# Value products of two key tiles in a row, with a third slot of probabilities

## The reference

```python
x = L0_attn_encoding                                    # 4 x 1024 x 128
xn = _layernorm(x)
x = x + causal_attention(xn, R) + mixture16(xn)         # one head; 16 experts, 2 per token
xn = _layernorm(x)
x = x + attention16(xn) + block(xn)

def attention16(x):                                     # 16 heads of width 8, no mask
    scores = q @ k.T / sqrt(8)
    attn = softmax(scores)                              # over all 1024 keys
    return (attn @ v) @ w_o
def block(x):                                           # 16 heads of width 4, causal,
    x = x + causal_heads(rmsnorm(x)) @ w_up             # then a mixture of 8 experts
    return x + mixture8(rmsnorm(x))
```

## Time and profile before

| | |
|---|---|
| median of 3 runs | 2106.05 us (2105.44 to 2109.2) |
| profiled execution: its own time on the page (span, first to last instruction) | 2106.5 us |
| PE busy | 2004.6 us, 95% |
| DVE busy | 1449.5 us, 69% |
| ACT busy | 1212.8 us, 58% |
| POOL busy | 248.6 us, 12% |
| mean granted clock of TensorE | 0.970 |

### The profile page before, as it was taken

One profiled execution on the slowest core, in us unless ns is written; L12 is line 12 of the kernel. 1 busy time (PEld: TensorE's weight loads), 2 busy tenths in 40 slices (PEclk: granted clock), 3 DMA queues, 4 the chain that ended last, 5 costly groups with the idle time before them and its releaser, 6 DMA issues.

```text
span 2106.5 us, 37548 instructions
## 1 busy us (share of the span) xinstructions
PE 2004.6 (95%) x14520; PEld 956.8 (45%) x14520; DVE 1449.5 (69%) x2024; ACT 1212.8 (58%) x2207; POOL 248.6 (12%) x376
## 2 busy tenths in 40 slices
PE   6989999999999999999899999999989999999899
PEld 3753233344765523344566542334456633334455
DVE  6758887673777688766577778876357888867232
ACT  2341677777442367788544156778864266777621
POOL 0022000000013300000002310000003300000034
PEclk9987999999999999999999999999999999999989
DMA  5244101000155010010116301001005310000011
GB/s 195 67 129 111 28 7 32 25 18 3 61 152 123 16 31 16 27 31 5 35 49 186 80 7 31 16 18 33 3 26 150 91 26 14 29 19 17 2 51 40
DMA packets 66643, 105.29 MB, mean 50 GB/s; under 512 B 11137, under 2 KB 20417, under 8 KB 66081
## 3 DMA queue, kind: packets, MB, share of 16 engines
q1 hardware_dynamic: 66464, 102.90, 17.7%
HBM read 79.13 MB, written 22.94 MB: 48 GB/s over the span
## 4 chain that ended last, share of the span: by engine, by line
PE 83%; DVE 7%; ACT 3%; issue 2%; DMA 2%; SPq 2%; POOL 1%; POOLq 0%; ACTq 0%; DVEq 0%
PE ps L1835 19%; PE ps L1805 16%; PE ps L1760 10%; PE ps L1669 8%; PE ps L1705 7%; PE ps L1695 7%; PE ps L1764 4%; DVE row_max L1295 2%; PE ps L1846 2%; PE ps L1747 2%; DVE row_max L1299 1%; PE ps L1620 1%; PE ps L1608 1%; ACT prob L1508 1%; PE ps L1584 1%
## 5 line engine op out<-in xcount | busy, mean ns | idle before, releaser
L1508 ACT ACTIVATE prob<-ps 128x512 f32<-128x512 f32 (+1 forms) x1664 | 854.7, 584 | 283.6 <-PE ps L1805 227.1
L1295 DVE TENSOR_REDUCE row_max<-ps 128x1 f32<-128x1024 f32 x512 | 606.6, 1219 | 123.1 <-PE ps L1760 121.5
L1805 PE MATMUL ps<-q_stack,k_stack 96*128 96x512 bf16 (+4 forms) x1792 | 493.5, 366 | 12.2 <-ACT prob L1508 6.9
L1835 PE MATMUL ps<-prob,v_ones 128*32 128x512 f32 (+3 forms) x4608 | 463.1, 477 | 2.6 <-ACT prob L1508 0.8
L1760 PE MATMUL ps<-k_stack,q_stack 96*128 96x512 bf16 x1024 | 320.6, 398 | 11.9 <-DVE row_max L1295 10.4
L1299 DVE TENSOR_REDUCE row_max<-ps 128x2 f32<-128x1024 f32 (+3 forms) x256 | 258.6, 1021 | 83.2 <-PE ps L1764 51.0
L1805 PEld LDWEIGHTS ps<-q_stack,k_stack 96*128 96x128 bf16 (+1 forms) x1792 | 140.7, 96 | 324.8 <-ACT prob L1508 190.7
L1448 ACT ACTIVATE prob<-ps 128x512 f32<-128x512 f32 x146 | 87.0, 597 | 345.3 <-PE ps L1695 341.2
L1008 POOL TENSOR_TENSOR prob<-prob,spread_w 128x512 f32<-128x512 f32 x144 | 187.1, 1300 | 540.8 <-DVE prob L1180 247.1
L1669 PEld LDWEIGHTS ps<-wd,prob 128*128 128x128 f32 (+1 forms) x1600 | 208.1, 193 | 73.7 <-issue 52.4
L1669 PE MATMUL ps<-wd,prob 128*128 128x128 f32 (+1 forms) x1600 | 213.9, 278 | 6.2 <-POOL prob L1008 6.2
(11 more groups left out here) (178 smaller groups left out, 1598.7 us busy)
## 6 DMA issues: line engine op xcount, KB each, us to landing
spread_w<-scratch_r SPq DMA_DIRECT2D x128, 128.0 KB, 2.9
spread_w<-scratch_r SPq DMA_DIRECT2D x64, 256.0 KB, 3.3
k_stack<-scratch_k SPq DMA_DIRECT2D x48, 256.0 KB, 6.4
q_stack<-scratch_q SPq DMA_DIRECT2D x48, 256.0 KB, 7.1
scratch_k<-tmp SPq DMA_DIRECT2D x36, 256.0 KB, 4.2
k_stack<-scratch_k SPq DMA_DIRECT2D x96, 64.0 KB, 2.3
q_stack<-scratch_q SPq DMA_DIRECT2D x96, 64.0 KB, 2.3
scratch_k<-tmp SPq DMA_DIRECT2D x36, 128.0 KB, 2.6
```

Source lines behind the costliest of these rows:

```text
L1295: dve.tensor_reduce(nm[G % 2][:, t, j], ring_pair(r)[:], AX_X, ALU.max).then_inc(s["ring_used"], 1)
L1508: act.activation(to, src, ACT.Exp, scale=SCALES[kind_of(G)]).then_inc(s["p_ready"], 1)
L1805: ins[n] = pe.matmul(dst[n][:, to], keys(G, head)[:, kc * P:(kc + 1) * P], queries(G, head)[:, lo:hi], start=k == 0, stop=True, skip_group ...
L1835: ins = pe.matmul(bank(V_BANK)[CW * j:CW * (j + 1), first - at:end - at], v_st[G % 2][:, kc, j, :], p_slot(v, j)[:, first - at:end - at], ...
```

## The change

1. `SLOTS_P = 3`: `prob` gets a third slot, and quads take the slots 0, 2, 1 in turn, counted from the batch's first quad. Exponentials of quad v wait for the value products of quad v-3 in place of v-2.
2. The four `spread_w` tiles no longer have memory of their own; they lie in the third slot (`SPREAD_SLOT`). The first four loads of a mixture that run behind a batch's heads wait for the last value product that read that slot.
3. Value products of full heads are placed two quads at a time: quad 2n and 2n+1 together, once the exponentials of both are there (`follows`). In the planner the second costs no fixed 0.19.

```diff
+SLOTS_P = 3
+SPREAD_SLOT = 2
 def values_time(kind, q, part):
     lo, hi = values_parts(kind, q)[part]
-    return 0.19 + (hi - lo) * 1.7e-3
+    return (0.0 if follows(kind, q) else 0.19) + (hi - lo) * 1.7e-3
+def follows(kind, q):
+    return kind == 0 and q % 2 == 1
+def slot_of(v):
+    return (0, SPREAD_SLOT, 1)[(v - QUAD0[PER * batch_of(group_of_quad(v))]) % SLOTS_P]
+def slot_free_at(v):
+    return max(v - SLOTS_P + 1, QUAD0[PER * batch_of(group_of_quad(v))])
...
-                if G in ready and quads.index((G, q)) < len(values_end) + 2:
+                if G in ready and quads.index((G, q)) < len(values_end) + SLOTS_P:
...
-                if not (opens and evacuating):
-                    starts["values"] = max(exp_end[G, q], staged[-1] if opens else 0.0) + LAT
+                last_of = q + 1 if (G, q + 1) in quads and follows(kind_of(G), q + 1) else q
+                if not (opens and evacuating) and (G, last_of) in exp_end:
+                    starts["values"] = max(exp_end[G, last_of], staged[-1] if opens else 0.0) + LAT
...
+                more = True
+                while more:
...
+                    more = False
+                    if part == len(values_parts(kind_of(G), q)):
+                        part = 0
+                        values_end.append(pe)
+                        more = (G, q + 1) in quads and follows(kind_of(G), q + 1)
...
-        prob = sb("prob", 2 * GH * HALF)
-        p_slot = lambda v, j: prob[:, (v % 2 * GH + j) * HALF:(v % 2 * GH + j + 1) * HALF]
+        prob = sb("prob", SLOTS_P * GH * HALF)
+        p_slot = lambda v, j: prob[:, (slot_of(v) * GH + j) * HALF:(slot_of(v) * GH + j + 1) * HALF]
-        spread_w = [sb(f"spread_w{n}", HALF) for n in range(SPREADS)]
+        spread_w = [prob[:, (SPREAD_SLOT * GH + n) * HALF:(SPREAD_SLOT * GH + n + 1) * HALF] for n in range(SPREADS)]
...
+                if which == 0 and b >= 2 and i < SPREADS:
+                    sp.wait_ge(s["pv_done"], max(v for v in range(QUAD0[PER * (b - 1)]) if slot_of(v) == SPREAD_SLOT) + 1)
...
-                if v >= 2:
-                    act.wait_ge(s["pv_done"], v - 1)
+                if slot_free_at(v) > 0:
+                    act.wait_ge(s["pv_done"], slot_free_at(v))
```

More of the change, by code:

```diff
@@ L123, in values_time, with group_of_quad @@
     lo, hi = values_parts(kind, q)[part]
-    return 0.19 + (hi - lo) * 1.7e-3
+    return (0.0 if follows(kind, q) else 0.19) + (hi - lo) * 1.7e-3
+def follows(kind, q):
+    return kind == 0 and q % 2 == 1
+def group_of_quad(v):
+    return int(np.searchsorted(QUAD0, v, side="right")) - 1
+def slot_of(v):
+    return (0, SPREAD_SLOT, 1)[(v - QUAD0[PER * batch_of(group_of_quad(v))]) % SLOTS_P]
+def slot_free_at(v):
+    return max(v - SLOTS_P + 1, QUAD0[PER * batch_of(group_of_quad(v))])
 def maximum_time(cols):
@@ L288, in windows @@
             elif what == "values":
[L289 to L298 removed]
+                more = True
+                while more:
+                    G, q = quads[len(values_end)]
+                    half, kc, lo, hi = QUADS[kind_of(G)][q]
+                    self.add("values", G, q, part)
+                    pe += values_time(kind_of(G), q, part)
+                    part += 1
+                    more = False
[3 more added lines that the diff above has]
+                        more = (G, q + 1) in quads and follows(kind_of(G), q + 1)
+                        if (G, q + 1) not in quads or QUADS[kind_of(G)][q + 1][0] > half:
+                            evacuating.append((pe, G, half))
             elif what == "piece":
@@ L1007, in spread @@
                 pool.wait_ge(s["down_done"], k - 1)
-                pool.tensor_tensor(hid[k % 2][:], gu[k % 2][:], spread_w[load % SPREADS][:], ALU.mult).then_inc(s["hid_ready"], 1)
+                pool.tensor_tensor(hid[k % 2][:], gu[k % 2][:], spread_w[load % SPREADS], ALU.mult).then_inc(s["hid_ready"], 1)
             for what, *how in plan.of("POOL"):
@@ L1193, in spread @@
                     dve.wait_ge(s["down_done"], k - 1)
-                dve.tensor_tensor(hid[k % 2][:], gu[k % 2][:], spread_w[load % SPREADS][:], ALU.mult).then_inc(s["hid_ready"], 1)
+                dve.tensor_tensor(hid[k % 2][:], gu[k % 2][:], spread_w[load % SPREADS], ALU.mult).then_inc(s["hid_ready"], 1)
             added, attended = [0] * B, [0] * B
```

18 lines of the change are left out of this document (4 added, 14 removed).

## The result

The changed kernel takes 2141.98 us, median of four runs (2135.15 to 2147.93), against 2107.62 for the kernel before, measured beside it: 1.0158 times as long, 95% interval [1.0141, 1.0175]. It is slower by 34 us where 18 were forecast, and 2 us above the end of the range. The profiled execution is the fastest of the four: 2135.15 us, 26.9 us more span than before. (A run's time is some 1.8 us longer than its span, here 2135.15 against 2133.4; the span of the kernel before, 2106.5, is compared with spans alone.) Its mean granted clock is 0.971; the others, at 0.967, 0.966 and 0.963, took 2140.60, 2143.36 and 2147.93. The 45 runs of the kernel before that stand beside the experiments lie between 2104.6 and 2114.6 at 0.969 to 0.975.

The account below looks back on a forecast made before the run. PE was taken as the bound, with little slack on DVE. Full-head terms 9.9 - 0.5 + 8.6 + 1.7 - 1.9, others 0, gave +17.8 us on a median of 2106.05: 2124 us, range 2100 to 2140.

Parts of the forecast that it names:

- The mechanism and the full heads: Full heads: a joint block of 1.86 us leaves DVE without pieces, and PE then waits for it; +17.8 us.
- the interval: Full heads, commonest stretch from one paired block to the next: 5.87 us against 5.66 before, +0.21 each.
- Outputs: Full heads, eight intervals whose output transposes take ring slots and wait for DVE: 6.74 us, +0.42 each.
- three pieces: Full heads, nine intervals with three pieces and seven units: 4.95 us against 5.01, -0.5 us together.
- The eight other intervals with outputs: Full heads, remaining intervals with output transposes: +0.70 us for four and +0.61 for four.
- The rule on weight loads: Joined blocks: unhidden loads, 108 ns per pass, would take 28 of 30.7 us saved; the prediction found the trace disagreed.
- Rival 1: Whole kernel: PE stays the bound and the ring never makes it wait; 2076 us, chance 0.09.
- Rival 3: Full heads: ACT's exponentials bind in place of DVE, 5.61 us with the piece first; 2100 us, chance 0.07.
- Rival 2: Full heads lose 17.8 us, but the mixed stretch (-9.6) and causal heads (-8) give it back; 2106 us, chance 0.17.
- Rival 4: Holes also open in the mixed stretch (+8.4) and causal heads (+8), beyond full heads; 2140 us, chance 0.12.
- Full units with causal pieces: Group 4 and the end of group 3, 40 pairs: DVE and PE level, 0 taken; ends -9.6 and +8.4 us.
- The third slot and causal heads: Causal heads: exponentials may run a quad further; 0 taken from PE's small gaps, ends -8 and +8 us.

Follow-up runs that it names:

- e3: The changed kernel with causal heads planned with two slots instead of three; 1.0171 times the kernel before.
- e8: The changed kernel with the last piece and last unit before a pair of value blocks swapped, 53 times; 1.0143 times the kernel before.
- e10: The changed kernel without pairs in group 4 of a batch, third slot planned everywhere; 1.0168 times the kernel before.
- e11: The changed kernel with pairs and third slot planned only in groups 1 to 3 of a batch; 1.0106 times the kernel before.
- e9: The changed kernel's memory, planned without pairs, third slot planned only in groups 5 and 6 of a batch; 1.0072 times the kernel before.
- e12: The changed kernel's memory, planned without pairs, third slot planned only in group 5 of a batch; 1.0001 times the kernel before.
- e6: The changed kernel with exponentials of full heads over 256 of 512 columns, maxima whole; 1.0113 times the kernel before.
- e7: The changed kernel with full heads' maxima over 512 of 1024 columns and exponentials over 256 of 512; 0.9864 times the kernel before.
- e4: The changed kernel with maxima of full heads over 512 of 1024 columns; 0.9967 times the kernel before.
- e2: The changed kernel planned without pairs, third slot kept in the plan for all groups; 1.0062 times the kernel before.
- e5: The kernel before with maxima of full heads over 512 of 1024 columns; 0.9953 times the kernel before unedited.

## Why the prediction was right or wrong

**The mechanism and the full heads: right, and shown.** The working gave 5.87 for the interval; the trace has 5.88. Outputs: 6.74 expected, 6.74 measured; three pieces 4.95, and 4.96. The eight other intervals with outputs (+0.70 and +0.61, given without their length) measure 7.80 and 6.79. The timeline of one with outputs:

```profile
292.70 0.59 PE L1834 MATMUL ps<-q_stack,k_stack 96*128 96x512 bf16 x2
293.63 0.63 PE L1875 MATMUL ps<-const_f,tmp 128*128 128x128 f32 x4 [0.33 <-DVE row_max L1324]
...
296.28 1.07 PE L1864 MATMUL ps<-prob,v_ones 128*32 128x512 f32 x8
```

The +17.8 for all of these stands against +18.9 in groups 1 to 3 of this execution, and 19.9 to 21.0 in e3, e8, e10 and e11. That 18.9 comes so near is partly luck: in these groups the changed execution ran 20.4 us at the lower level, the one before 30.6, and at 0.33 us for each, as in e9 and e12 (2.2 for 6.8), 3 us of loss are hidden by it. In the first batch, where e3, e6 and e10 have as much of it as before, the three groups lose 4.5, or 18.1 in four batches; with 0.33 put back for each us that is missing, the changed kernel, e3, e10 and e11 all come to 22, of which the kernels without pairs show up to 1.7 by themselves. The intervals are right, then, and the sum is short by 0 to 4 us that no run places. The block behaved as worked out: PE's next matmul comes 1.86 after its start (283.66 to 285.52), so the entry and the exit of one block were saved. The rule on weight loads in the Trainium skill (TensorE: Matmul & The Clock Gate, What overlaps and what doesn't), that they overlap matmuls in flight only where the row group differs, would make the block some 2.08 (an estimate: 1.86 and two loads of 108 ns); the trace disagrees again, and e7's 5.41 leaves no room for it.

**Rival 1, PE stays the bound: refuted.** e7 shows that its 5.41 is there when maxima and exponentials take less time, e4 that the maxima are what stood in the way. **Rival 3, ACT: refuted as the bound** by e6, but its number was good: it gave 5.61 where ACT alone binds and the piece is first, and e4 shows 5.64. **Rival 2, the hole is given back in the mixed stretch and causal heads: refuted**; these parts added 9.4 us instead of taking 17.6 away. **Rival 4, holes in the mixed stretch and causal heads too:** its 2140 is the number nearest to the result, and that is chance. Group 4 added 2.1 where it has 8.4; the 7.3 behind it are near its 8, but causal heads have no pairs and so no such holes; its sum would be 34 in one execution, and 26.9 were measured.

**Full units with causal pieces: 0 was forecast.** Group 4 adds 2.1, inside the bounds of -9.6 and +8.4. In e10 and e11, without pairs in it, it adds 1.8: the pairs themselves cost 0.3 there, as good as the 0 of the forecast, and the rest is there without them.

**The term that was mis-sized: "The third slot and causal heads", taken as 0.** Alone it measures +9.6 + 4.5 = +14 (e2), beyond the +8 that I gave as its end; in the changed kernel groups 5 to 8 and the mixtures add 7.3. The step that failed was to take the value from PE's small gaps before, "nearest to the small gaps of the first stretch", as though a freer planner could only use gaps up. A third slot changes which work is done first: units before pieces, so that the maxima of the batch's last group end later, and there a chain of 8 us has to be covered by what is left. That chain was in the trace of before, at 478.68 to 486.59, and PE was covered to 0.6 us of it. e2 and e9 show this loss. In the changed kernel it is there too, smaller: the loads of group 8's first unit wait 1.23,

```profile
490.85 0.10 PEld L1834 LDWEIGHTS ps<-q_stack,k_stack 48*128 48x128 bf16 x2 [1.23 <-DMA q_stack<-tmp]
```

and group 7 adds 0.77 per batch. More of the 7.3 lies in group 5, 1.2 per batch, of which e11, with the order of before there, still has 0.45; what makes the rest no run shows.

**The second part of the miss is the clock.** The sum was made against one execution and moved to the median by 0.45. The changed kernel's profiled execution is 6.8 us under its median, and its four runs order by the granted clock, 0.971 to 0.963. By these means and the spans that is 35 us more at the lower level for 12.8 us of time, 0.36 for each, an estimate between the 0.33 of e9 and the 0.43 of e11: so the clock accounts for the spread. Why it falls more often in this kernel is argued, not shown: more waits of PE give more places at which it can fall. What supports it is that lower-level stretches turn up in groups 3 to 7, where the kernel before had none (e11 at 423.1, 13.7 us long; the changed kernel at 1860.6, 3.4 us), and that the kernels with the worst turn in group 8 (e2, e9, e10) have the lowest clocks, 0.960 to 0.968 in their twelve runs.

Together: 17.8 forecast; +1.1 in groups 1 to 3; +2.1 in group 4; +7.3 behind it; -1.4 ahead of the first group; that is the profiled execution's 26.9. The other 6.8 to the median is what other executions of the changed kernel take more. The last 2.2 up to 2141.98 are an error of the sum's ending: it set a span of 2106.5 beside a median of times, 2106.05, and called the difference 0.45. The span belongs to an execution of some 2108.3 (1.8 more), which is 2.2 above that median.

**Still open:** why group 8 and the mixtures differ so between batches of the same kernel (-1.6, +0.4, +3.3, -0.9 in the changed one). The time at the lower level there changed by -3.4, +6.9, +6.9 and -2.4 us, which goes with all but the second; no experiment separated the clock from the loads there.

## What to carry to other kernels

When two blocks of work are joined on an engine that feeds others through a short ring, work out the ring's hole first: here DVE had work for 1.45 us from the block's start and got its next piece at 2.7, and a joint block of 1.86 us turned an engine that idled 19% of the time (67.00 busy of 83.00) into the bound. Halving one consumer's work at a time gives each engine's own interval in three runs, and says at once what a joined block would be worth. More room in a buffer that a greedy planner sees is a change of order, not only of waits: look for the longest chain behind the item that is now done last.

## What the runs showed that I had not expected

- Ahead of the very first head group 22 pieces stand in a row, bound by VectorE. Timeline of DVE, the kernel before and e5:

```profile
161.88 26.26 DVE L1295 TENSOR_REDUCE row_max<-ps 128x1 f32<-128x1024 f32 x22 [0.19 <-PE ps L1760]
```

```profile
166.43 11.21 DVE L1295 TENSOR_REDUCE row_max<-ps 128x1 f32<-128x512 f32 x16
```

  A maximum takes 1.19 us of it and 0.70 with half of the columns, and the first group starts 13.3 us earlier in e5. The clock goes with it; windows of both (167 to 193 us):

```profile
167.00:193.00 26.00, 22.57 (x44) 4.14 (x45) 24.68 (x23) 0.32 (x1) 2.47 (x2) 0.54 0.51 138
```

```profile
167.00:193.00 26.00, 24.49 (x103) 10.54 (x103) 19.61 (x31) 2.39 (x4) 7.75 (x11) 1.00 0.60 149
```

  PE shows 22.57 of 26 us busy at a granted clock of 0.54 while it waits for DVE at every second piece: the busy share is high because two matmuls of a piece start 0.40 apart where 0.216 is usual. Why the clock is at the lower level there for 23.9 us and in e5 not at all is not shown; PE's waits for DVE are what e5 takes away. It is the one place in the kernel before where shorter maxima alone were worth 13 us.
- 13.7 us at the lower of the two levels cost 5.9 us in a stretch in which PE is busy 99% of the time (e11, group 5), 0.43 us for each; 6.8 us at the seam behind group 1 cost 2.2 (e9, e12), 0.33 for each.
- Two value blocks joined: the four passes over 512 columns start 0.45, 0.43 and 0.43 us apart (16 matmuls), with no gap between the second quad's loads and the first's matmuls.
